# Reading two PSUM banks with one instruction: a reduction and an exponential over a pair of banks

## The chip, the cores and the metric

One core of one Trainium2 chip runs the whole kernel. The time is that of one execution on the device, in microseconds (us); the kernel before was run three times for it, and once more under the hardware profiler.

## What is computed

Two transformer blocks over 16 batches of 256 tokens, 128 channels each. Every block normalizes its input, runs an attention and a mixture of 8 experts (top 2) on it, and adds attention times silu(experts) to the input. Layer 0 has a causal attention with two softmaxes per head whose difference is taken; layer 1 has a window of 128 keys. Cut to the part around the change:

```python
# layer 0: 16 heads of size 8, causal, two score sets
att1 = softmax(where(causal, q1 @ k1.T * scale, -inf))
att2 = softmax(where(causal, q2 @ k2.T * scale, -inf))
y = (att1 - lam * att2) @ v            # then a norm over each head, then @ c_w
# layer 1: 16 heads of size 8, keys t-127 .. t
attn = softmax(q @ window(k).T / sqrt(8))
ctx = attn @ window(v)
```

## The kernel before

The kernel runs its stages one after another: layer norm, router, experts, attention, twice. The change lies in `build_attention` alone, which is built for each layer.

**Scores twice.** The attention computes the scores of a batch twice. The first pass is row by row (queries on the partitions): VectorE takes the maximum of each row of a head (`search`, L1277), and the negated maximum, the shift, is turned and written by DMA as two more rows into the stacked queries in SBUF (`fill_shift`, L935). The second pass, for the following batch's turn, is transposed (keys on the partitions) and has the shift already in the sum, so that ScalarE only has to take exp (`exp`, L1182) into `probs`, from which TensorE weighs the values (`weigh`, L1062).

**Units and banks.** A batch has UNITS units: 12 in layer 0 (A = 2 score sets), 6 in layer 1. In unit n of a step TensorE fills two banks `s_bank[0..1]` with scores for the maximum of a batch further on (AHEAD is 4 units plus a batch in layer 0, 3 plus a batch in layer 1), and two banks `t_bank[0..1]` with transposed scores of this batch, the matmuls of the two kinds alternating (`both_scores`, L1042, called for i = 0 and i = 1). A PSUM bank has 512 fp32 columns on each of 128 partitions. Matmuls L986 add the masks, L987 the products. There are 16, 20 or 24 of them in a unit that has both kinds.

**Who waits for whom.** `s_full` and `t_full` are counted up once per bank, as are `s_free` and `t_free`: before TensorE fills bank i of unit n it waits until VectorE and ScalarE have read bank i of unit n - 1, not the other one. The wait is

```python
lone_wait(pe, s_free, b * BANKS + (2 * m + i - 1))
lone_wait(pe, t_free, step * BANKS + (2 * n + i - 1))
```

**The order within a step.** All engines run the same written-out order, step by step and unit by unit, and every queue is in order. After the scores of unit n TensorE does in that unit: `weigh` (16 matmuls, L1077 and L1080) in units n = 0 and 1 (for the last group of the step before) and in n = 3, 4, 6, 7, 9, 10 of layer 0 and n = 3, 4 of layer 1; and the general work of the table ORDER. In layer 0: two turnings of weighed values at n = 2 (L1088), the projection of v at n = 4 (L975), of queries and keys at n = 5 and 6 (L968), the turned shift (L1103) and two more turnings at n = 8, and at n = 11 the turned rows (L1096, which waits for GpSimd) and the output projection (L1112). In layer 1: qk at n = 0 and 1, turnings at n = 2, the shift at n = 3, v and rows at n = 4, out at n = 5. ScalarE copies each of these results out of PSUM after the exponentials of the same unit. VectorE's order in a unit is: maxima, then `negate` (L1290), `twice_silu`, `split_shift` (L1306), `divide` (L1316) and the parts of `split` (L1265). In layer 0 `divide` is at n = 3 (second score set of the batch before) and n = 9, and the parts of `split` (L1269, L1272, L1275, 1024 columns wide) at n = 7, 8, 9.

**Two loops beside the units.** In layer 0 GpSimd normalizes the rows of the batch before (`head_norm`, L832: from L854 to L867), which begins after the `divide` of n = 3 and is awaited by L1096 at n = 11. In layer 1 the stacked queries and keys are written by 12 DMAs per batch from SyncE's queue (`fill_stack`, L924, issues on L933), after `fill_shift` in the same queue; ScalarE's copy of the next projection (`copy_qk`, L1162) waits for them and stands ahead of the exponentials of unit n = 1.

Of the kernel before, what the change touches and what calls it, by code (L numbers as in the profile page):

```python
# [6 lines left out]
ALU = mybir.AluOpType  # L7
ACT = mybir.ActivationFunctionType
AX = mybir.AxisListType
# [5 lines left out]
P = 128  # L15
# [11 lines left out]
SCALE = 1.0 / math.sqrt(HD)  # L27
# [13 lines left out]
SLOTS = HEADS // 2  # L41
# [615 lines left out]
def build_attention(nc, R, D, layer):  # L657
# [8 lines left out]
    A = 2 if layer == 0 else 1  # L666
# [6 lines left out]
    UNITS = 6 * A  # L673
    BANKS = 2 * UNITS
# [23 lines left out]
    def has(step, name):  # L698

        if not isinstance(step, int):  # L700
            return True
        if name.startswith("qk"):
            return 0 <= step + 3 <= LAST
        if name in ("v", "shift"):
            return 0 <= step + 1 <= LAST
        if name in ("rows", "out", "last", f"turn{A - 1}0", f"turn{A - 1}1"):
            return 0 <= step - 1 <= LAST
        return 0 <= step <= LAST
# [3 lines left out]
    def maxima_of(step, n):  # L712

        batch, m = (step + 1, n + AHEAD) if n + AHEAD < UNITS else (step + 2, n + AHEAD - UNITS)
        if isinstance(batch, int) and not 0 <= batch <= LAST:
            return None
        return batch, m
# [8 lines left out]
    with ExitStack() as ctx:  # L726
        sem = lambda name: ctx.enter_context(nc.semaphore(f"at{layer}_{name}"))

        def sb(name, shape, dt=F32):
            return ctx.enter_context(nc.sbuf_tensor(f"at{layer}_{name}", shape, dt))  # L730
# [5 lines left out]
        maxima = sb("maxima", [P, QB, A * HEADS])  # L736
# [3 lines left out]
        probs = sb("probs", [P, 2, 3, 1024])  # L740
# [29 lines left out]
        s_full, s_free = sem("s_full"), sem("s_free")  # L770
# [3 lines left out]
        t_full, t_free = sem("t_full"), sem("t_free")  # L774
# [22 lines left out]
        stack = R.stack  # L797
        G = [R.ps[:, i, :] for i in range(2)]
        s_bank, t_bank = ([R.ps[:, 2 * u + i, :] for i in range(2)] for u in (1, 2))
        Y = [R.ps[:, 6 + i, :].rearrange("p (f s) -> p f s", f=2) for i in range(2)]  # L800

        def bank_of(step, name):
# [7 lines left out]
        def lone_wait(eng, s, value):  # L810

            if not (isinstance(value, int) and value <= 0):
                eng.wait_ge(s, value)
                eng.sem_inc(passed, 1)
# [144 lines left out]
        def _(pe):  # L959
# [35 lines left out]
            def scores_for_max(j, batch_r, n, i):  # L995


                a, r = divmod(n, 6)
                q, k = (stack_of(batch_r, a, tensor) for tensor in range(2))
                late = int(r >= 2)  # L1000
                per, w = 4 // (late + 1), P * (late + 1)
                if j >= per + 2:
                    return None
                h0 = (r - 2 * late) * per
                if not late:
                    fine, mask = one_block(0), R.mask_diag_q[:]
                elif layer == 0:
                    fine, mask = one_block(P), R.mask_diag_q[:, 0:2, :]
                else:
                    fine, mask = two_blocks, R.mask_late_q[:]  # L1010
                ins = score_matmul(j, s_bank[i], i, per, SHIFT_ROW, fine, mask,
                                   lambda m: q[:, h0 + m, late * P:(late + 1) * P], lambda m: k[:, h0 + m, 0:w])
                if j == per + 1:
                    ins.then_inc(s_full, 1)
                return ins
# [26 lines left out]
            def both_scores(step, r, n, i):  # L1042

                ahead = maxima_of(step, n)
                now = has(step, "now")
                if ahead:
                    b, m = ahead
                    if m == 0 and i == 0:
                        pe.wait_ge(stacked, b * LOADS + LOADS)
                    lone_wait(pe, s_free, b * BANKS + (2 * m + i - 1))  # L1050
                if now:
                    if n == 0 and i == 0:

                        pe.wait_ge(shift_in, step * SHIFTS + SHIFTS)
                    lone_wait(pe, t_free, step * BANKS + (2 * n + i - 1))
                for j in range(6):
                    if ahead:
                        scores_for_max(j, r + 1 if n + AHEAD < UNITS else r + 2, m, i)
                    if now:
                        scores(j, r, n, i)  # L1060

            def weigh(b, p, g, part):  # L1062

                a, group = divmod(g, 2)
                if part == 0:
                    pe.wait_ge(t_free, b * BANKS + 6 * (g + 1))

                    lone_wait(pe, y_free, b * GROUPS + (g - 1))
                pr = probs[:, g % 2]
                for late in range(2):  # L1070
                    for j in range(STRIPS):
                        h = group * 8 + part * 4 + j
                        i, m = 1 - j // 2, j % 2
                        strip = Y[g % 2][j * VW:(j + 1) * VW, part, :]
                        if not late:
                            at = i * 512 + m * SEQ
                            nc.tensor.matmul(strip, v[p][:, 0, h, :], pr[:, part, at:at + SEQ], start=True, stop=False)  # L1077
                        else:
                            at = i * 512 + (part * 2 + m) * P
                            last = nc.tensor.matmul(strip[:, P:SEQ], v[p][:, 1, h, :], pr[:, 2, at:at + P], start=False, stop=True)  # L1080
                last.then_inc(weighed, 1)
# [69 lines left out]
        def _(act):  # L1151
# [30 lines left out]
            def exp(b, n):  # L1182
                if n % 3 == 0:

                    lone_wait(act, weighed, b * (2 * GROUPS) + 2 * (n // 3 - 1))
                for i in range(2):
                    act.wait_ge(t_full, b * BANKS + (2 * n + i + 1))
                    nc.scalar.activation(probs[:, (n // 3) % 2, n % 3, i * 512:(i + 1) * 512], t_bank[i], ACT.Exp, scale=SCALE).then_inc(t_free, 1)  # L1188

            def copy_weighed(b, g):  # L1190
                act.wait_ge(weighed, b * (2 * GROUPS) + 2 * (g + 1))

                nc.scalar.copy(weighed_t[:, g // 2, g % 2, :, :], Y[g % 2]).then_inc(y_free, 1)  # L1193

# [69 lines left out]
        def _(dve):  # L1264
# [12 lines left out]
            def search(b, n):  # L1277
                a, r = divmod(n, 6)
                late = int(r >= 2)
                heads = 4 // (late + 1)  # L1280
                if n == 0:
                    lone_wait(dve, shift_ready, b)
                for i in range(2):
                    h0 = i * SLOTS + (r - 2 * late) * heads
                    dve.wait_ge(s_full, b * BANKS + (2 * n + i + 1))
                    by_half = maxima[:, late, :].rearrange("p (h a) -> p h a", a=A)
                    nc.vector.tensor_reduce(by_half[:, h0:h0 + heads, a], s_bank[i].rearrange("p (m k) -> p m k", k=P * (late + 1)),  # L1287
                                            AX.X, ALU.max).then_inc(s_free, 1)

            def negate(b, p):  # L1290
                dve.wait_ge(s_free, b * BANKS + BANKS)
                if layer:

                    nc.vector.tensor_scalar(maxima[:, 0, :], maxima[:, 0, :], R.no_outside[:, 0:1], None, ALU.max).then_inc(max_ready, 1)
                    dve.wait_ge(max_ready, b + 1)
                if layer == 0:
                    nc.vector.tensor_scalar(shift[p][:], maxima[:], -1.0, None, ALU.mult).then_inc(shift_ready, 1)
                else:

                    nc.vector.tensor_scalar(high[:], maxima[:], -1.0, None, ALU.mult).then_inc(round_chain, 1)  # L1300
                    dve.wait_ge(round_chain, b * 2 + 1)
                    nc.vector.scalar_tensor_tensor(out=low[:], in0=maxima[:], scalar=-1.0, in1=high[:], op0=ALU.mult, op1=ALU.subtract).then_inc(round_chain, 1)
                    dve.wait_ge(round_chain, b * 2 + 2)
                    nc.vector.tensor_tensor(shift[p][:], high[:], low[:], ALU.add).then_inc(shift_ready, 1)
# [67 lines left out]
def build(nc, D):  # L1372
    D["list_in"] = nc.dram_tensor("list_in", (TILES * P, C), F32).ap()
    D["list_out"] = nc.dram_tensor("list_out", (TILES * P, C), F32).ap()
    with ExitStack() as ctx:
# [38 lines left out]
        for layer in range(2):  # L1414
            build_layernorm(nc, R, layer)
            build_router(nc, R, layer)
            build_experts(nc, R, D, layer)
            build_attention(nc, R, D, layer)
# [37 lines left out]
```

## Time and profile before

| | us |
|---|---|
| median of 3 runs | 1562.79 |
| lowest and highest | 1559.96, 1567.36 |
| the profiled execution | 1560.15 |
| its span (first to last instruction) | 1558.4 |

Busy shares of the span: TensorE 69%, VectorE 51%, ScalarE 49%, GpSimd 42%. The attention of layer 0 runs from about 327 us to 890 us with its tail, that of layer 1 from about 1194 us to the end; between and before them lie the experts. In the rows below, PE is TensorE matmuls, PEld its weight loads, DVE VectorE, ACT ScalarE, POOL GpSimd, SP SyncE.

### The profile page before, as it was taken

What the parts mean: (1) busy time and instruction counts of PE and PEld (TensorE: products, weight loads), DVE (VectorE), ACT (ScalarE), POOL (GpSimd) and SP (SyncE); (2) the same over time, 40 slices, a digit from 0 to 9 for tenths busy, and PEclk for the clock granted to TensorE, in tenths of its full rate; (3) what the DMA queues carried; (4) which work ended last, traced back from release to release, by engine and by line L of the source; (5) the groups of instructions that cost most, each with busy time, mean ns of one, the idle gap of its engine ahead of it and who ended that gap; (6) DMA issues with size and microseconds to landing.
All of it is one profiled execution on the core that took longest, in us unless ns stands there. A gap on an engine that the chain in (4) does not pass through costs nothing. (4 is left out here: it accounts for less than half of the span.)

```text
span 1558.4 us, 39725 instructions
## 1 busy us (share of the span) xinstructions
PE 1080.5 (69%) x12282; PEld 821.1 (53%) x12282; DVE 797.8 (51%) x1739; ACT 756.5 (49%) x1764; POOL 652.9 (42%) x868
## 2 busy tenths in 40 slices
PE   1400899858888788888888233009996678888886
PEld 1400899835655556555654122009996355555564
DVE  5411466447667666567562054115663555555561
ACT  2070456415667566676667022005553255555564
POOL 2277100010577677677767721760002013333344
PEclk9999999958899889898898555559998599999997
DMA  6061222132322232222400002312222222222220
GB/s 175 6 191 51 63 67 69 51 88 51 83 50 51 51 86 61 51 50 58 89 10 9 7 0 85 100 55 61 67 68 58 55 50 62 63 56 59 63 55 25
DMA packets 166094, 95.52 MB, mean 61 GB/s; under 512 B 18547, under 2 KB 159749, under 8 KB 165957
## 3 DMA queue, kind: packets, MB, share of 16 engines
q1 hardware_dynamic: 157764, 76.82, 19.0%
q0 software_dynamic: 8192, 16.79, 3.8%
q8 instruction: 96, 1.57, 0.4%
q14 instruction: 42, 0.34, 0.1%
HBM read 30.19 MB, written 24.64 MB: 35 GB/s over the span
## 5 line engine op out<-in xcount | busy, mean ns | idle before, releaser
L1287 DVE TENSOR_REDUCE at_maxima<-ps 128x2 f32<-128x512 f32 (+1 forms) x576 | 372.4, 685 | 224.2 <-PE ps L987 222.2
L1188 ACT ACTIVATE at_probs<-ps 128x512 f32<-128x512 f32 x576 | 322.4, 602 | 103.2 <-PE ps L987 98.3
L986 PE MATMUL ps<-tables 64*128 64x256 bf16 (+1 forms) x2304 | 232.6, 265 | 121.9 <-DVE at_maxima L1287 50.1
L615 ACT ACTIVATE ex_hid<-ps,ex_w 128x128 f32<-128x128 f32 x576 | 164.4, 368 | 251.0 <-PE ps L585 251.0
L987 PE MATMUL ps<-stack 64*128 64x128 bf16 (+3 forms) x3072 | 269.6, 262 | 0.0
L986 PEld LDWEIGHTS ps<-tables 64*128 64x128 bf16 x2304 | 96.1, 98 | 224.5 <-issue 189.8
L987 PEld LDWEIGHTS ps<-stack 64*128 64x128 bf16 (+1 forms) x3072 | 171.2, 102 | 9.1
L577 PE MATMUL ps<-ident,ex_rows 128*128 128x128 f32 x144 | 40.2, 279 | 195.2 <-DMA ex_rows<-list_in 195.1
L522 POOL DMA_INDIRECT list_in<-ex_rows,ex_slots x128 | 125.1, 977 | 100.9 <-DVE ex_slots L628 63.4
L646 DVE COPY ex_w<-ex_weights 128x1156 f32 x144 | 109.9, 763 | 106.4 <-issue 106.4
L585 PE MATMUL ps<-ex_rowsT,ex_w 128*128 128x128 f32 x1152 | 158.3, 282 | 0.1
L595 PE MATMUL ps<-ex_w,ex_hid 128*128 128x128 f32 x1152 | 153.6, 277 | 1.2 <-DVE ex_result L653 1.2
L877 POOL DMA_INDIRECT at_chosen_y<-list_out,at_slot x128 | 124.8, 975 | 55.6 <-issue 28.9
L585 PEld LDWEIGHTS ps<-ex_rowsT,ex_w 128*128 128x128 f32 x1152 | 143.1, 196 | 2.3 <-issue 0.7
L595 PEld LDWEIGHTS ps<-ex_w,ex_hid 128*128 128x128 f32 x1152 | 141.6, 194 | 1.5 <-issue 1.5
L1077 PE MATMUL ps<-at_probs,at_v 128*32 128x256 f32 x1536 | 130.9, 414 | 0.0
L577 PEld LDWEIGHTS ps<-ident,ex_rows 128*128 128x128 f32 x144 | 21.1, 146 | 197.0 <-issue 197.0
L898 POOL TENSOR_TENSOR at_s_rows<-at_s_rows,at_silu 128x256 f32<-128x256 f32 x32 | 23.5, 734 | 194.5 <-ACT at_s_rows L1229 194.1
L864 POOL TENSOR_TENSOR at_rstd<-at_stat,at_half 128x32 f32<-128x32 f32 x16 | 89.2, 5574 | 2.9 <-POOL at_stat L862 2.9
L1080 PE MATMUL ps<-at_probs,at_v 128*32 128x128 f32 x1536 | 80.7, 283 | 0.0
L626 DVE COPY ex_rows<-xn 128x128 f32 (+1 forms) x64 | 15.2, 237 | 123.8 <-DMA list_in<-ex_rows,ex_slots 123.2
L1269 DVE TENSOR_TENSOR at_whole<-at_whole,at_pieces 128x1024 f32<-128x1024 f32 (+1 forms) x32 | 31.1, 972 | 91.5 <-ACT at_pieces L1170 69.9
(166 smaller groups left out, 1555.6 us busy)
## 6 DMA issues: line engine op xcount, KB each, us to landing
stack<-at_pieces SPq DMA_DIRECT2D x192, 128.0 KB
stack<-at_pieces SPq DMA_DIRECT2D x192, 64.0 KB, 2.0
ex_rows<-list_in SPq DMA_DIRECT2D x144, 64.0 KB, 1.8
list_out<-ex_result SPq DMA_DIRECT2D x144, 64.0 KB, 1.5
list_in<-zero_tile SPq DMA_DIRECT2D x1, 4608.0 KB, 17.7
ex_weights<-in_L_w SPq DMA_DIRECT2D x4, 1024.0 KB, 7.4
ex_weights<-in_L_w SPq DMA_DIRECT2D x16, 256.0 KB, 7.1
x<-in_L_attn_x SPq DMA_DIRECT2D x4, 512.0 KB, 6.3
```

What stands on the lines that cost most here:

```text
L522: nc.gpsimd.indirect_dma_start(D["list_in"], bass.IndirectOffsetOnAxis(slots[q][k][:], 0), rows[q][:], None).then_inc(scattered[q], 16)
L585: last = nc.tensor.matmul(hid_ps[q % 2][:, hb * P:(hb + 1) * P], w[q][:, W1 + hb * P:W1 + (hb + 1) * P], rowsT[q % 2][:], start=True, stop ...
L595: last = nc.tensor.matmul(out_ps[q % 2][:, 0:C], hid[q % 2][:, hb, :], w[q][:, W2 + hb * C:W2 + (hb + 1) * C], start=(hb == 0), stop=(hb = ...
L615: last = nc.scalar.activation(hid[q % 2][:, hb, :], hid_ps[q % 2][:, hb * P:(hb + 1) * P], gelu, bias=w[q][:, B1 + hb:B1 + hb + 1])
L646: nc.vector.tensor_copy(w[q][:], weights[:, bass.ds(e, 1), :].rearrange("p o w -> p (o w)"))
L864: nc.gpsimd.tensor_tensor(rstd[:], stat[:], half[:], ALU.pow).then_inc(rstd_ready, 1)
L877: nc.gpsimd.indirect_dma_start(chosen_y[t][k][:], None, D["list_out"], bass.IndirectOffsetOnAxis(slot[:, i:i + 1], 0)).then_inc(gathered, 16)
L986: return nc.tensor.matmul(fine(bank, j), R.eye[tile, j, :], mask[tile], start=(j == 0), stop=True, skip_group_check=(j > 0))
L987: return nc.tensor.matmul(bank[:, j - 2, :], left(j - 2)[tile], right(j - 2)[tile], start=False, stop=True, skip_group_check=True)
L1077: nc.tensor.matmul(strip, v[p][:, 0, h, :], pr[:, part, at:at + SEQ], start=True, stop=False)
L1188: nc.scalar.activation(probs[:, (n // 3) % 2, n % 3, i * 512:(i + 1) * 512], t_bank[i], ACT.Exp, scale=SCALE).then_inc(t_free, 1)
L1287: nc.vector.tensor_reduce(by_half[:, h0:h0 + heads, a], s_bank[i].rearrange("p (m k) -> p m k", k=P * (late + 1)), AX.X, ALU.max).then_inc ...
```

## The change

One maximum over both s banks of a unit (an access pattern of 2 x heads x keys, 1024 columns) takes the place of two, and one exponential over both t banks (1024 columns) of two. `s_free` and `t_free` are counted once per unit, VectorE and ScalarE wait until both banks are full, and TensorE waits once, ahead of i = 0, until both banks of unit n - 1 have been read. `s_full` and `t_full` stay per bank.

```diff
+        s_pair, t_pair = R.ps[:, 2:4, :], R.ps[:, 4:6, :]
...
-                    lone_wait(pe, s_free, b * BANKS + (2 * m + i - 1))
+                    if i == 0:
+                        lone_wait(pe, s_free, b * UNITS + m)
...
-                    lone_wait(pe, t_free, step * BANKS + (2 * n + i - 1))
+                    if i == 0:
+                        lone_wait(pe, t_free, step * UNITS + n)
...
-                    pe.wait_ge(t_free, b * BANKS + 6 * (g + 1))
+                    pe.wait_ge(t_free, b * UNITS + 3 * (g + 1))
...
-                for i in range(2):
-                    act.wait_ge(t_full, b * BANKS + (2 * n + i + 1))
-                    nc.scalar.activation(probs[:, (n // 3) % 2, n % 3, i * 512:(i + 1) * 512], t_bank[i], ACT.Exp, scale=SCALE).then_inc(t_free, 1)
+                act.wait_ge(t_full, b * BANKS + 2 * (n + 1))
+                nc.scalar.activation(probs[:, (n // 3) % 2, n % 3, :].rearrange("p (i k) -> p i k", i=2), t_pair, ACT.Exp, scale=SCALE).then_inc(t_free, 1)
...
-                for i in range(2):
-                    h0 = i * SLOTS + (r - 2 * late) * heads
-                    dve.wait_ge(s_full, b * BANKS + (2 * n + i + 1))
-                    by_half = maxima[:, late, :].rearrange("p (h a) -> p h a", a=A)
-                    nc.vector.tensor_reduce(by_half[:, h0:h0 + heads, a], s_bank[i].rearrange("p (m k) -> p m k", k=P * (late + 1)),
-                                            AX.X, ALU.max).then_inc(s_free, 1)
+                h0 = (r - 2 * late) * heads
+                dve.wait_ge(s_full, b * BANKS + 2 * (n + 1))
+                by_half = maxima[:, late, :].rearrange("p (i h a) -> p i h a", i=2, a=A)
+                nc.vector.tensor_reduce(by_half[:, :, h0:h0 + heads, a], s_pair.rearrange("p i (m k) -> p i m k", k=P * (late + 1)),
+                                        AX.X, ALU.max).then_inc(s_free, 1)
...
-                dve.wait_ge(s_free, b * BANKS + BANKS)
+                dve.wait_ge(s_free, b * UNITS + UNITS)
```

## Rows read from the trace of the kernel before

**Rows 1.** Stretch, length, then busy us (x) of PE, PEld, DVE, ACT, POOL; clock; DMA.
```profile
419.99:805.75 385.76, 328.32 (x4721) 221.73 (x4721) 251.09 (x417) 256.19 (x512) 277.00 (x336) 0.88 0.25 58
1262.90:1496.70 233.80, 194.87 (x2400) 131.18 (x2400) 136.59 (x293) 134.82 (x326) 86.06 (x143) 0.94 0.23 59
547.50:551.40 3.90, 3.13 (x14) 2.53 (x16) 0.00 (x0) 0.58 (x1) 2.45 (x4) 0.50 0.85 213
```

**Rows 2.** TensorE's waits in twelve layer-0 steps: waiter, awaited: total us, times, longest.
```profile
PE ps L986 <- DVE at_maxima L1287: 18.5, 11, 2.1
PE ps L1096 <- POOL at_out_rows L867: 11.3, 12, 2.5
```

**Rows 3.** Timeline, TensorE, one layer-0 step: start us, us, instruction, count [idle before].
```profile
551.37 0.40 PE L986 MATMUL ps<-tables 64*128 64x128 bf16 x4
...
552.19 0.64 PE L987 MATMUL ps<-stack 64*128 64x256 bf16 x4
...
559.61 0.29 PE L986 MATMUL ps<-tables 64*128 64x128 bf16 x4
...
562.47 0.28 PE L986 MATMUL ps<-tables 64*128 64x128 bf16 x3
...
564.41 0.29 PE L986 MATMUL ps<-tables 64*128 64x128 bf16 x4
...
567.02 0.29 PE L986 MATMUL ps<-tables 64*128 64x128 bf16 x4
...
567.48 0.38 PE L987 MATMUL ps<-stack 62*128 62x256 bf16 x4
...
568.85 0.40 PE L986 MATMUL ps<-tables 64*128 64x256 bf16 x4 [0.20 <-ACT at_probs L1188]
...
571.82 0.39 PE L986 MATMUL ps<-tables 64*128 64x256 bf16 x4
...
572.38 0.39 PE L987 MATMUL ps<-stack 62*128 62x128 bf16 x6
...
576.99 0.28 PE L986 MATMUL ps<-tables 64*128 64x128 bf16 x3 [1.64 <-DVE at_maxima L1287]
...
579.36 0.66 PE L1096 MATMUL ps<-ident,at_out_rows 128*128 128x128 f32 x4 [1.15 <-POOL at_out_rows L867]
...
582.25 0.40 PE L986 MATMUL ps<-tables 64*128 64x128 bf16 x4
```

**Rows 4.** Timeline of the same step, VectorE's maxima of units 7 and 10.
```profile
567.56 1.29 DVE L1287 TENSOR_REDUCE at_maxima<-ps 128x2 f32<-128x512 f32 x2 [1.33 <-PE ps L987]
...
576.01 1.28 DVE L1287 TENSOR_REDUCE at_maxima<-ps 128x2 f32<-128x512 f32 x2
```

**Rows 5.** Groups by shape, 1024 columns: count | busy us, mean ns | idle before.
```profile
L174 DVE TENSOR_REDUCE ln_total<-ln_sq 128x8 f32<-128x1024 f32 x8 | 9.8, 1220 | 9.0 <-ACT ln_sq L194 9.0
...
L194 ACT ACTIVATE ln_sq<-xn 128x1024 f32<-128x1024 f32 x8 | 8.4, 1056 | 50.3 <-DVE xn L170 50.3
```

**Rows 6.** Timeline of the same step, GpSimd's first and last operation of the norm.
```profile
561.41 1.27 POOL L854 TENSOR_TENSOR at_y<-at_y 128x512 f32<-128x512 f32 x1 [3.00 <-DVE at_y L1336]
...
578.25 1.06 POOL L867 TENSOR_TENSOR at_out_rows<-at_y,at_rstd 128x512 f32<-128x512 f32 x1 [0.18 <-POOL at_rstd L864]
```

**Rows 7.** Timeline of layer 1, units 2 to 4 of a step.
```profile
1322.58 0.40 PE L986 MATMUL ps<-tables 64*128 64x256 bf16 x4 [1.94 <-ACT at_probs L1188]
...
1324.78 1.28 DVE L1287 TENSOR_REDUCE at_maxima<-ps 128x2 f32<-128x512 f32 x2
...
1325.76 0.40 PE L986 MATMUL ps<-tables 64*128 64x256 bf16 x4 [0.85 <-DVE at_maxima L1287]
...
1328.01 1.28 DVE L1287 TENSOR_REDUCE at_maxima<-ps 128x4 f32<-128x512 f32 x2
```

**Rows 8.** VectorE's maxima before layer 0's first full step (group, 330.7 to 347.8 us).
```profile
L1287 DVE TENSOR_REDUCE at_maxima<-ps 128x2 f32<-128x512 f32 (+1 forms) x18 | 11.6, 686 | 2.7 <-PE ps L987 2.7
```

**Rows 9.** Timeline of layer 1's last steps, one unit's maxima.
```profile
1516.22 1.29 DVE L1287 TENSOR_REDUCE at_maxima<-ps 128x2 f32<-128x512 f32 x2 [0.48 <-PE ps L987]
```

## Prediction

> **What bounds the kernel now.** I read the busy shares first, by stretch: in the steady steps of layer 0 TensorE is busy 328 of 386 us and VectorE 251, in layer 1 TensorE 195 of 234 [rows 1]. No engine is full, so the order of hand-offs decides. Next the waits: in twelve steps of layer 0 TensorE stands 18.5 us for maxima (11 times) and 11.3 us for GpSimd's normalized rows (12 times, 0.94 each) [rows 2]. Then one step in order of time. TensorE's own work paces most units: unit 4 takes 2.86 us (559.61 to 562.47), unit 6 2.61 (564.41 to 567.02). Unit 7, with little but scores and weighing in it, takes 1.83 us, and TensorE waits only 0.20 us after it [rows 3]. In that unit VectorE starts on the first bank at 567.56, while TensorE fills the second until 567.86 (567.48 + 0.38), and ends at 568.85, when TensorE has just begun unit 8 [rows 3, 4]. So the two banks of a pair overlap the engines: one is read while the other is filled or not yet needed. The whole step, 551.37 to 582.25, takes 30.88 us.
>
> Two loops run beside this. In layer 0 GpSimd works at the norm from 561.41 to 579.31 (578.25 + 1.06), 17.9 us, and TensorE waits 1.15 us for it in unit 11, after its scores ended at 578.21 [rows 3, 6]. In layer 1 TensorE stands 1.94 us ahead of unit 2 for an exponential [rows 7]; by the order of ScalarE's queue that exponential is behind a copy that waits for SyncE's twelve DMAs. Units 5, 0 and 1 of layer 1 therefore have some 2 us of cover.
>
> **What the change removes.** One reduction in two and one exponential in two. Two maxima back to back take 1.28 to 1.29 us [rows 4]. A 1024-column reduction, from SBUF, takes 1.22 [rows 5]. It is the nearest row in length and in kind, so I take 1.22 for the pair; the bounds are 1.22 and 1.29. An exponential pair should take about the 1.06 of the 1024-column square [rows 5], which is below 1.22 and starts at the same moment; I cost it at nothing where VectorE has nothing else to do, because the reduction hides it. The dropped waits of TensorE I cost at nothing too: they free a stall of up to 0.3 us between the banks, counted below for unit 11.
>
> The Trainium skill, VectorE: DVE Perf Modes, section "The TRN2 errata", gives a PSUM read on VectorE a fixed 120 cycles besides one per element at 0.96 GHz, so one instruction in place of two would save 0.125 us. The rows say 0.07, since the second of two reductions overlaps the first one's end. By the page's figure the sum below would be some 5 to 10 us smaller; I keep the row.
>
> **What it adds.** TensorE may not touch either s bank of unit n + 1 until the single reduction has ended, and that reduction may not begin until both banks of unit n are full. The unit's period gets a floor: scores of both banks, the reduction, and the way back to TensorE. The terms:
> - Scores of both banks without a stall: 0.84 us with 16 matmuls (567.02 to 567.86), 0.95 with 20 (571.82 to 572.77) [rows 3]; 1.06 with 24 by the same step, an estimate. In unit 0 the matmuls run at the lower clock and take 1.46 (551.37 to 552.83) [rows 3].
> - The reduction: 1.22.
> - The way back: a maximum starts at 1324.78, one bank takes 0.686 [rows 8], TensorE starts at 1325.76 [rows 7]: 0.29, say 0.3.
>
> The floors are 2.36 us (16), 2.47 (20), 2.58 (24) and 2.98 (unit 0). What is queued behind TensorE's wait is the scores, and behind them the weighing and the general work, which cannot move ahead. Unit by unit in layer 0, with the step shown [rows 3]:
> - Units 0 to 3: 8.24 us now (551.37 to 559.61), 2.98 + 2.36 + 2.58 + 2.47 = 10.39 after: +2.15.
> - Units 4 and 6: own work of 2.86 and 2.61 exceeds the floor: 0.
> - Unit 5: 1.94 now (562.47 to 564.41), 2.47 after: +0.53. Unit 7: 1.83 to 2.36: +0.53.
> - Unit 8: 2.97 now (568.85 to 571.82). Its second turning waits for ScalarE's shift copies, which are queued behind an exponential that now starts at about 1.1 us in place of 0.7. Bounds 0 and 0.4; I take +0.2.
> - Units 9 and 10: 5.17 now (571.82 to 576.99). VectorE's two maxima of unit 9 would run from about 572.5 to 573.8, and unit 10's start at 576.01 without idle [rows 4], so 2.25 us of its other work lie between. After: unit 9 takes 2.47; its reduction ends 2.17 into it; unit 10's starts 2.25 later, 1.95 into unit 10, and that unit takes 1.95 + 1.22 + 0.3 = 3.47. Sum 5.94: +0.77.
> - Unit 11: its scores take 1.22 now (576.99 to 578.21), 0.95 without the wait between banks: -0.27.
>
> That is +3.9 us. From it goes the cover: TensorE arrives later at the rows that it now awaits 0.94 us on average [rows 2]. Does GpSimd stay ahead? Its norm starts after unit 3's maxima, and those end 2.17 into the unit in place of some 1.95. From there to the end of unit 11's scores TensorE would need 0.3 + 2.86 + 2.47 + 2.61 + 2.36 + 3.17 + 5.94 + 0.95, about 20.7 us, GpSimd its 17.9 and VectorE's division of some 1.5 ahead of it, 19.4. So GpSimd is ready first and the cover is used up: **+3.0 us a step**, 13 steps between full ones: +39.
>
> The rest, by the same floor: before the first full step VectorE's maxima alone set the pace, nine pairs in 14.3 us of busy and idle time, 1.6 a pair [rows 8]. There the floor is about 1.1 (two banks at the lower clock, an estimate) + 1.22 + 0.3 = 2.6, +1.0 for 9 or 10 units: +9. The end of layer 0, exponentials without maxima: +3. Layer 1: its start, six units: +3. Its middle, 12 steps: TensorE starts unit 3 about 0.55 us later, but VectorE is busy until unit 3's maxima anyway (1324.78 to 1326.06, again from 1328.01 without idle [rows 7]), so the shift and SyncE's DMAs hardly move, and the 1.94 us at unit 2 takes up the rest: +2, bounds 0 and 6. Its last steps, where no loop waits: a unit's maxima come every 1.77 us (1.29 + 0.48) [rows 9] and would come every 1.05 + 1.22 + 0.3 = 2.6 (scores of 1.05 at layer 1's width, by bounds 0.95 and 1.1), some seven units: +6.
>
> **The sum.** 39 + 9 + 3 + 3 + 2 + 6 = +62 us against the profiled execution's 1560.15: 1622. The median of the runs lies 2.6 above that execution, so 1625.
>
> **The rivals.**
> - *Milder.* GpSimd's norm goes on setting layer 0's step, or TensorE's clock recovers in units 11 and 0 because it no longer stands ahead of the rows. Then a step gains only the start of the norm's delay, about +1.9, or loses the 1.2 us that the lower clock costs there: 13 x 1.8 + 12 = +35, 1598. For it: stalls at 0.50 clock are seen just there [rows 1]. Against it: the count above puts GpSimd 1.3 us ahead.
> - *The clock falls.* Every unit now has an idle of 0.5 to 0.9 us. If that keeps TensorE at 1.2 GHz, scores take 1.46 in place of 0.84 and eight floors of a step grow by 0.62: 13 x 5 + some 20 in layer 1, about 1710. Against it: around the idle 0.85 and 1.94 us in layer 1 the matmul groups keep their 0.40 us [rows 7], and that stretch runs at 0.94 [rows 1]; at the lower clock such groups last longer (0.64 against 0.38 [rows 3]). The Trainium skill, TensorE: Matmul & The Clock Gate, section "A second HAM failure mode: psum-queue depth-cycling", tells of a kernel whose short idle times between groups made the clock swing. By that rule this case would come true; the rows of layer 1 do not show it.
> - *Not slower.* TensorE's other work covers the reduction in every unit, and the shorter reading tells: 0.07 us on 288 pairs is at most -20 us, 1543, and with part of it covered, no change. It decides where the work after the scores reaches 1.5 us. Units 4 and 6 reach it; units 1, 2, 3, 5, 7 and 9 don't, with periods under 2.1 [rows 3].
>
> **How the numbers follow.** The floor with its covers 0.70; milder 0.13; the clock 0.08; not slower 0.09, of which within 0.5% (about what this kernel's runs can tell) 0.05 and faster 0.04. The range takes in the first two: below, cover in full and clock recovery with the start smaller, 1590; above, the reduction at 1.29 (+6), the way back or the queues of units 8 to 10 worse by 0.5 us each (+20), and the lower clock in a few more units (+20), 1670.
>
> **What would show it.** Right: TensorE's waits for maxima rise from 18.5 us in twelve steps to 60 or more; a plain unit's period is 2.3 to 2.5; one reduction lasts 1.22; the wait for rows in unit 11 is gone; layer 1's middle steps keep about 20 us. Wrong: unit 7 stays under 2 us (the floor is not there); L1096 still waits 1 us or more (GpSimd sets the pace); the granted clock in layer 0 falls below 0.8 from 0.88; or layer 1's steps grow by over a us, which would mean that SyncE's DMAs start later.

## The result and the profile after

| | before | after |
|---|---|---|
| median | 1562.41 us (4 runs, 1559.96 to 1567.36) | 1635.03 us (4 runs, 1633.72 to 1638.12) |
| ratio, 95% interval | | 1.0475 [1.0452, 1.0498] |
| span of the profiled execution | 1558.4 | 1632.5 |

The change makes the kernel 4.75% slower, +72.6 us. The forecast was 1625, with 1590 to 1670 around it.

The page of the changed kernel, its part with the costliest groups (line, engine, operation, count | busy us, mean ns | idle before):

```profile
L1288 DVE TENSOR_REDUCE at_maxima<-ps 128x4 f32<-128x1024 f32 (+1 forms) x288 | 352.2, 1223 | 324.9 <-PE ps L988 323.8
L1190 ACT ACTIVATE at_probs<-ps 128x1024 f32<-128x1024 f32 x288 | 295.1, 1025 | 252.7 <-PE ps L988 251.7
L987 PE MATMUL ps<-tables 64*128 64x256 bf16 (+1 forms) x2304 | 223.5, 263 | 228.7 <-DVE at_maxima L1288 144.0
```

The fused instructions do what they should: a reduction of 1024 columns takes 1.223 us and an exponential 1.025. But VectorE, whose busy time fell, is idle 324.9 us ahead of its reductions, and TensorE stands 144.0 us for them. They now wait for each other in turn.

Lines L986, L987, L1287 and L1188 of before are L987, L988, L1288 and L1190 here; L1088, L1096 and L1112 (the turnings and the output projection) are L1091, L1099 and L1115. Stretches of the changed kernel: the way to unit 11 of step 1 in layer 0, twelve steps of layer 0, its end, and eleven steps of layer 1 (columns as in [rows 1]):

```profile
327.44:435.41 107.97, 68.04 (x870) 43.97 (x871) 63.84 (x65) 43.07 (x66) 15.53 (x16) 0.75 0.19 46
435.41:865.73 430.32, 314.16 (x4721) 218.03 (x4722) 242.35 (x273) 238.76 (x368) 276.18 (x336) 0.92 0.24 54
865.73:919.72 53.99, 38.96 (x622) 25.69 (x623) 17.55 (x24) 34.26 (x51) 38.75 (x54) 1.00 0.05 12
...
1339.50:1565.12 225.62, 181.46 (x2289) 126.16 (x2290) 126.29 (x209) 126.31 (x243) 87.00 (x143) 0.95 0.24 60
```

The first two and the last of these stretches in the kernel before, cut at the same instructions (TensorE's first matmul of unit 11 in layer 0, of unit 5 in layer 1); the end of layer 0 took 56.66 us there:

```profile
327.47:413.85 86.38, 71.36 (x871) 45.39 (x871) 65.73 (x103) 45.49 (x89) 13.29 (x14) 0.79 0.24 58
413.85:798.61 384.76, 329.21 (x4721) 222.50 (x4722) 251.19 (x418) 255.65 (x512) 275.86 (x337) 0.87 0.26 60
...
1273.57:1496.73 223.16, 185.20 (x2289) 124.10 (x2289) 129.11 (x275) 127.82 (x309) 86.06 (x143) 0.95 0.24 61
```

The start of layer 0 costs 21.6 us, its twelve steps 45.6 (3.8 a step), its end gives back 2.7. Layer 1's eleven middle steps cost 2.5, its start and its end 3.9 and 5.5. That makes 76.3 us; the stretches between the layers and at the very end give back the remaining 2.2 of the spans' 74.1. The granted clock in the twelve steps did not fall, it rose from 0.87 to 0.92. With the same matmuls TensorE is busy 15.1 us less there (329.21 and 314.16) and idle 60.6 us more: part of what the new waits cost comes back through the clock.

One step's units 7, 10 and 11 in the changed kernel, TensorE:

```profile
527.40 0.29 PE L987 MATMUL ps<-tables 64*128 64x128 bf16 x4
...
529.80 0.40 PE L987 MATMUL ps<-tables 64*128 64x256 bf16 x4 [0.77 <-ACT at_probs L1190]
...
535.71 0.29 PE L987 MATMUL ps<-tables 64*128 64x128 bf16 x4 [0.81 <-DVE at_maxima L1288]
...
539.18 0.29 PE L987 MATMUL ps<-tables 64*128 64x128 bf16 x3 [1.84 <-DVE at_maxima L1288]
...
540.06 0.66 PE L1099 MATMUL ps<-ident,at_out_rows 128*128 128x128 f32 x4
```

and VectorE in the same units, then GpSimd:

```profile
528.27 1.22 DVE L1288 TENSOR_REDUCE at_maxima<-ps 128x4 f32<-128x1024 f32 x1 [1.39 <-PE ps L988]
...
536.53 1.22 DVE L1277 TENSOR_TENSOR at_pieces<-at_whole,at_pieces 128x1024 bf16<-128x1024 f32 x1
537.66 1.22 DVE L1288 TENSOR_REDUCE at_maxima<-ps 128x4 f32<-128x1024 f32 x1
```

```profile
537.20 1.46 POOL L868 TENSOR_TENSOR at_out_rows<-at_y,at_rstd 128x512 f32<-128x512 f32 x1 [0.18 <-POOL at_rstd L865]
```

Unit 7 now takes 2.40 us (1.83 before [rows 3]). Its reduction starts at 528.27, 0.87 into the unit, not at 0.54 [rows 4]; it ends at 529.49 and TensorE goes on at 529.80. The row names ScalarE's exponential, which ended at 529.51, a reminder that a wait for two is put down to one. In unit 11 TensorE no longer waits for the rows: GpSimd's last operation ended at 538.66, 1.4 us before TensorE came for them (1.15 us after it had come, before [rows 3, 6]).

TensorE's waits in the twelve steps (waiter, awaited: total us, times, longest), after and then before:

```profile
PE ps L987 <- DVE at_maxima L1288: 71.7, 81, 2.0
PE ps L1115 <- ACT at_yT L1204: 12.6, 12, 1.1
PE ps L1091 <- ACT at_shift_p L1219: 10.9, 11, 1.0
PE ps L987 <- ACT at_probs L1190: 9.4, 12, 0.9
```

```profile
PE ps L986 <- DVE at_maxima L1287: 20.0, 12, 2.1
PE ps L1096 <- POOL at_out_rows L867: 9.4, 12, 1.2
PE ps L1112 <- ACT at_yT L1202: 9.2, 12, 0.8
PE ps L1088 <- ACT at_shift_p L1217: 6.0, 11, 0.5
```

Waits for maxima rise from 20.0 us in 12 waits to 71.7 in 81; the 9.4 us for the rows are gone; two waits for ScalarE's copies grow.

### The profile page after: what moved, and what is told of

Its sections match the earlier page's. It is cut to its first block and busy times, and to the rows that moved or that the text cites. A ratio compares the mean times of both kernels' runs of the same rounds, so it can differ in the third digit from the quotient of the medians.

```text
span 1632.5 us, 37908 instructions
## 1 busy us (share of the span) xinstructions
PE 1051.3 (64%) x12282; PEld 813.3 (50%) x12282; DVE 782.2 (48%) x1451; ACT 731.3 (45%) x1476; POOL 653.3 (40%) x868
## 5 line engine op out<-in xcount | busy, mean ns | idle before, releaser
L1288 DVE TENSOR_REDUCE at_maxima<-ps 128x4 f32<-128x1024 f32 (+1 forms) x288 | 352.2, 1223 | 324.9 <-PE ps L988 323.8
L1190 ACT ACTIVATE at_probs<-ps 128x1024 f32<-128x1024 f32 x288 | 295.1, 1025 | 252.7 <-PE ps L988 251.7
L987 PE MATMUL ps<-tables 64*128 64x256 bf16 (+1 forms) x2304 | 223.5, 263 | 228.7 <-DVE at_maxima L1288 144.0
L987 PEld LDWEIGHTS ps<-tables 64*128 64x128 bf16 x2304 | 107.9, 98 | 316.3 <-issue 289.5
L988 PE MATMUL ps<-stack 62*128 62x256 bf16 (+3 forms) x3072 | 254.1, 260 | 3.6 <-issue 3.6
L988 PEld LDWEIGHTS ps<-stack 62*128 62x128 bf16 (+1 forms) x3072 | 166.9, 101 | 11.0 <-issue 4.2
L855 POOL TENSOR_TENSOR at_y<-at_y 128x512 f32<-128x512 f32 x16 | 20.4, 1275 | 176.2 <-DVE at_y L1337 175.9
```

Source lines behind the costliest of these rows:

```text
L987: return nc.tensor.matmul(fine(bank, j), R.eye[tile, j, :], mask[tile], start=(j == 0), stop=True, skip_group_check=(j > 0))
L988: return nc.tensor.matmul(bank[:, j - 2, :], left(j - 2)[tile], right(j - 2)[tile], start=False, stop=True, skip_group_check=True)
L1190: nc.scalar.activation(probs[:, (n // 3) % 2, n % 3, :].rearrange("p (i k) -> p i k", i=2), t_pair, ACT.Exp, scale=SCALE).then_inc(t_free, 1)
L1288: nc.vector.tensor_reduce(by_half[:, :, h0:h0 + heads, a], s_pair.rearrange("p i (m k) -> p i m k", k=P * (late + 1)), AX.X, ALU.max).then ...
```

## The experiments

The theory under test: a pair of banks lets TensorE fill one while VectorE reads the other, and reading both with one instruction ends that. Each unit gets a floor of scores, reduction and way back. Rivals: the wide instructions cost in themselves; each fused instruction costs its share; TensorE's clock; GpSimd's norm still sets the step. In the table below all ratios are to the kernel before on the same chip.

| | edit | us | ratio, 95% interval |
|---|---|---|---|
| 1 | maxima fused only | 1628.91 | 1.0415 [1.0381, 1.0449] |
| 2 | exponentials fused only | 1586.64 | 1.0140 [1.0096, 1.0184] |
| 3 | the change's waits, two instructions | 1646.20 | 1.0522 [1.0487, 1.0557] |
| 4 | only TensorE's wait is once | 1588.51 | 1.0156 [1.0123, 1.0189] |
| 5 | change, split part 3 later | 1606.50 | 1.0296 [1.0263, 1.0328] |
| 6 | before, split part 3 later | 1558.90 | 0.9994 [0.9976, 1.0012] |
| 7 | fused in covered units | 1561.82 | 1.0021 [1.0002, 1.0039] |
| 8 | fused in the others | 1644.81 | 1.0546 [1.0515, 1.0578] |
| 9 | change, TensorE waits per bank | 1656.83 | 1.0614 [1.0589, 1.0639] |
| 10 | the changed kernel again | 1636.29 | 1.0492 [1.0477, 1.0506] |

The kernel before had a median of 1563.83 beside 1 to 4, 1559.99 beside 5 to 8 and 1559.28 beside 9 and 10; 1 to 4 ran on one chip, 5 to 10 on another.

**1. Maxima fused only.**

```diff
-                    lone_wait(pe, s_free, b * BANKS + (2 * m + i - 1))
+                    if i == 0:
+                        lone_wait(pe, s_free, b * BANKS + 2 * m)
...
+                nc.vector.tensor_reduce(by_half[:, :, h0:h0 + heads, a], s_pair.rearrange("p i (m k) -> p i m k", k=P * (late + 1)),
+                                        AX.X, ALU.max).then_inc(s_free, 2)
```

> Only the maxima are read as a pair (TensorE waits once per unit on s, per bank on t; exponentials per bank). Theory, the lost overlap of two banks: the floor of a unit is scores 0.84 + reduction 1.22 + way back 0.3, and the exponential pair was hidden inside it, so nearly the whole cost is here: 65 to 75 us above the kernel before (it was +73 with both), ratio 1.042 to 1.048. Rival, each fused instruction costs its own share: about half, +36 us.

Measured: 1.0415, +65 us. As the theory had it: some nine tenths of the cost come with the maxima alone.

**2. Exponentials fused only.**

```diff
-                    lone_wait(pe, t_free, step * BANKS + (2 * n + i - 1))
+                    if i == 0:
+                        lone_wait(pe, t_free, step * BANKS + 2 * n)
...
+                nc.scalar.activation(probs[:, (n // 3) % 2, n % 3, :].rearrange("p (i k) -> p i k", i=2), t_pair, ACT.Exp, scale=SCALE).then_inc(t_free, 2)
```

> Only the exponentials are read as a pair. Theory: a floor of 0.84 + 0.05 + 1.02 + 0.14 = 2.05 us for a unit of 16 matmuls against some 1.6 to 1.8 before, partly covered by GpSimd's norm: about 1.0 us a step of layer 0, and some 3 us in each layer's last steps: +15 to +30 us. With the first kernel the two must add to more than the change's +73, since the floors hide each other. Rival, additive shares: +36 us here and +36 there.

Measured: 1.0140, +23 us. Equal shares for the two instructions are out. The two add to 88, not 73, as the theory wants, in which ScalarE's shorter floor hides behind VectorE's; the waits of the changed kernel agree (in layer 0's twelve steps TensorE's scores wait 81 times for maxima and 12 times for exponentials). But the sum alone does not prove it: kernels 1 and 2 each keep one of TensorE's two waits per bank, which the change drops, and kernel 9 will show that such waits have a cost of their own.

**3. The change's waits, two instructions each.** Both readers wait for both banks, TensorE waits once (its part of the edit is that of kernel 4, below).

```diff
...
-                    act.wait_ge(t_full, b * BANKS + (2 * n + i + 1))
+                    act.wait_ge(t_full, b * BANKS + 2 * (n + 1))
...
-                    dve.wait_ge(s_full, b * BANKS + (2 * n + i + 1))
+                    dve.wait_ge(s_full, b * BANKS + 2 * (n + 1))
```

> Two reductions and two exponentials per unit as before, but VectorE and ScalarE start only when both banks are full and TensorE waits once for both: the waits of the change without its wide instructions. Theory: the cost is the waits, and two reductions take 1.29 where one takes 1.22, so this is slower than the changed kernel by 0.07 us for each unit at the floor: +5 to +15 us over it, ratio 1.050 to 1.057. Rival, the wide access pattern across two banks costs in itself: near the kernel before.

Measured: 1.0522, +82 us. The cost is there without any wide instruction. So the wide access pattern is not what costs. Against two instructions under the same waits it looks worth 5 to 7 us (1.0475 and, in kernel 10, 1.0492), but the intervals overlap, so that gain is not shown. VectorE's pairs in this kernel:

```profile
530.10 1.29 DVE L1289 TENSOR_REDUCE at_maxima<-ps 128x2 f32<-128x512 f32 x2 [1.17 <-PE ps L987]
```

1.29 us where one instruction takes 1.22.

**4. Only TensorE's wait is once per unit.** The readers start on each bank as it fills.

```diff
-                    lone_wait(pe, s_free, b * BANKS + (2 * m + i - 1))
+                    if i == 0:
+                        lone_wait(pe, s_free, b * BANKS + 2 * m)
...
-                    lone_wait(pe, t_free, step * BANKS + (2 * n + i - 1))
+                    if i == 0:
+                        lone_wait(pe, t_free, step * BANKS + 2 * n)
```

> Instructions per bank, each starting when its own bank is full as before; only TensorE's wait is once per unit, for both banks. Theory: the first reduction starts 0.54 us into a unit of 16 matmuls and not 0.88, so the floor is 0.54 + 1.29 + 0.3 = 2.13 us and not 2.36: between a third and half of the cost, +20 to +35 us. Rival, TensorE's single wait is the whole of it and the start of the readers does not matter: +65 or more.

Measured: 1.0156, +25 us. A unit of 20 matmuls in it:

```profile
517.18 0.39 PE L986 MATMUL ps<-tables 64*128 64x256 bf16 x4
...
519.42 0.29 PE L986 MATMUL ps<-tables 64*128 64x128 bf16 x4 [0.50 <-DVE at_maxima L1289]
```

```profile
517.83 1.29 DVE L1289 TENSOR_REDUCE at_maxima<-ps 128x4 f32<-128x512 f32 x2 [0.31 <-PE ps L987]
```

The first bank is read from 0.65 us on (517.83), both are free at 519.12, TensorE starts at 519.42: 2.24 us, where the changed kernel has 2.5 to 2.6 for such a unit. Added in this order, the cost splits: about a third is TensorE's waiting for both banks to be free, two thirds (kernel 3 less kernel 4, 57 us) are the readers' waiting for both to be full. The other order, readers alone, was not run.

**5 and 6. One 1024-column subtraction of VectorE moved from unit 9 to unit 10 of layer 0**, in the changed kernel and in the kernel before.

```diff
-        SPLIT = {7: (0,), 8: (1,), 9: (2,)}
+        SPLIT = {7: (0,), 8: (1,), 10: (2,)}
```

> The changed kernel with one 1024-column subtraction of VectorE (the third part of split, layer 0) moved from unit 9 to unit 10, behind unit 10's maxima. Theory: in the changed kernel TensorE's own path through the units sets layer 0's step, and GpSimd's rows are ready 1.4 us before TensorE comes for them, so what is taken off unit 10 (3.46 to about 2.4 us) is gained whole: -1.0 us for each of 13 steps, -10 to -14 us. Rival, GpSimd's norm or the DMAs still set the step: 0 to -3 us.

> The same move in the kernel before. Theory: there TensorE already waits 0.94 us in unit 11 for GpSimd, so the 1.2 us taken off unit 10 turns into a longer wait for the rows: 0 to -4 us. Rival, TensorE's path sets the step here too: -12 us or more.

Measured: the changed kernel drops to 1.0296, 28 us less than in its own comparison (1.0475) and 30 less than kernel 10; the kernel before stays, 0.9994 with 1 inside the interval. TensorE's waits for the rows in the twelve steps of kernel 6, and units 10 and 11 in kernel 5:

```profile
PE ps L1096 <- POOL at_out_rows L867: 26.6, 12, 2.3
```

```profile
529.48 0.29 PE L987 MATMUL ps<-tables 64*128 64x128 bf16 x4 [0.81 <-DVE at_maxima L1288]
...
531.88 0.28 PE L987 MATMUL ps<-tables 64*128 64x128 bf16 x3 [0.77 <-DVE at_maxima L1288]
```

In the kernel before, what TensorE saves ahead of unit 11 it stands longer for GpSimd (26.6 us for 9.4): GpSimd's norm sets that step. In the changed kernel the same move is gained, so there TensorE's path sets it and the cover was used up. It is gained twice over, and the expectation (10 to 14 us) had only the first half. Unit 10 took 2.40 us in place of 3.46. And the twelve steps fell from 430.32 to 407.74, 1.9 a step, while their granted clock went from 0.92 to 0.96:

```profile
432.00:839.74 407.74, 299.83 (x4720) 207.87 (x4721) 246.72 (x274) 238.62 (x368) 275.68 (x336) 0.96 0.25 57
```

TensorE's busy time separates the two. Of the 22.6 us, 8.3 are idle time and 14.3 are shorter matmuls (299.83 for 314.16, the same instructions). TensorE's idle ahead of unit 11 went from 1.84 to 0.77 us, and the output projection that follows is where the difference is largest, in the changed kernel and then in kernel 5, the same step:

```profile
541.86 2.04 PE L1115 MATMUL ps<-wo,at_yT 128*128 128x128 f32 x8 [1.15 <-ACT at_yT L1204]
```

```profile
534.56 1.13 PE L1115 MATMUL ps<-wo,at_yT 128*128 128x128 f32 x8 [1.14 <-ACT at_yT L1204]
```

Over the twelve steps these matmuls take 411 ns each in the changed kernel and 319 in kernel 5. So the second half is TensorE running at its higher level (2.4 GHz) for more of each step; that the shorter idle ahead of unit 11 is what brings this about is the likely reading, and no run isolates it.

**7 and 8. Fused by unit.** Kernel 7 fuses where TensorE's own work is longer than the reduction, kernel 8 everywhere else.

```diff
+    FUSED = {4, 6} if layer == 0 else {4, 5}
...
+                if (n - AHEAD) % UNITS in FUSED:
...
+                if n in FUSED:
```

In kernel 8 the first line is

```diff
+    FUSED = set(range(UNITS)) - ({4, 6} if layer == 0 else {4, 5})
```

> The pair is read by one instruction only in the units whose other TensorE work is longer than the reduction (4 and 6 of layer 0, 4 and 5 of layer 1), per bank elsewhere. Theory: no floor is reached, so nothing is lost, and the shorter reading is worth 0.07 us at most in a few units: within 0.5% of the kernel before, 0 to -4 us. Rival, every pair costs: 24% of the change, about +15 us.

> The complement: pairs in all units but 4 and 6 of layer 0 and 4 and 5 of layer 1. Theory: the whole cost sits here, +68 to +76 us over the kernel before, as with the change. Rival, every pair costs alike: +55 to +60 us.

Measured: kernel 7 at 1.0021, 2 us above, where every pair costing alike would give 15; kernel 8 at 1.0546, +85 us. The cost lies in the units where the floor is reached; that every pair costs alike is out. Two misses. Kernel 7 was expected at 0 to -4 us and shows no gain from the shorter reading: where it is covered it is worth nothing either. And kernel 8 was expected at +68 to +76; with fewer fused units than the change it is slower than it by 8 to 11 us. It differs from the change in TensorE's waits, which stand ahead of each bank in all units, and this led to the next kernel.

**9. The change with TensorE's waits left per bank**, and 10, the changed kernel beside it. Both counts go up by two at once, so in i = 1 the wait is already met.

```diff
-                    if i == 0:
-                        lone_wait(pe, s_free, b * UNITS + m)
+                    lone_wait(pe, s_free, b * BANKS + (2 * m + i - 1))
...
-                    if i == 0:
-                        lone_wait(pe, t_free, step * UNITS + n)
+                    lone_wait(pe, t_free, step * BANKS + (2 * n + i - 1))
```

> The changed kernel, but TensorE keeps its waits ahead of each bank (both counts go up by two with one instruction, so the second pair of waits is met before it is reached). Kernel 8 showed units of 16 matmuls whose readers start 0.94 us into them and not 0.88. Theory: a wait that is already met costs TensorE about 0.06 us between the banks, on the path in some nine units a step: +7 to +12 us over the changed kernel, ratio about 1.053. Rival, met waits are free: the changed kernel's time within 3 us.

> The changed kernel itself on the same chip, to compare kernel 9 with: ratio 1.0475 as before, 1.045 to 1.050.

Measured: 1.0614 against 1.0492, 20.5 us more, beyond the expected 7 to 12. Met waits are not free here. A unit of 16 matmuls that begins at 619.61 (kernel 9):

```profile
619.61 0.28 PE L987 MATMUL ps<-tables 64*128 64x128 bf16 x4
...
622.08 0.40 PE L987 MATMUL ps<-tables 64*128 64x256 bf16 x4 [0.84 <-DVE at_maxima L1286]
```

```profile
620.56 1.23 DVE L1286 TENSOR_REDUCE at_maxima<-ps 128x4 f32<-128x1024 f32 x1 [1.41 <-PE ps L988]
```

Its reduction starts 0.95 us into the unit, 0.87 in the changed kernel, and the unit takes 2.47 us and not 2.40. Seven hundredths in nine units of 13 steps are 8 us. The whole is more because the other units lose too: on average over eleven steps units 1 to 10 are each 0.08 to 0.24 us longer than in kernel 10. The twelve steps differ by 11.3 us (442.38 and 431.1); the other 9 lie outside them and were not taken apart. Each dropped wait goes with a count of its own, and which of the two costs was not tried.

## Why the prediction was right

**The floor.** It was the likeliest case, and it is what happened. Predicted 2.36 us for a plain unit, measured 2.40 (unit 7); the terms: scores 0.84 and 0.84, reduction 1.22 and 1.22, way back 0.3 and 0.31 (529.49 to 529.80). A hand-off of some hundredths from TensorE to VectorE, left out of the sum, is the 0.03 left. Unit 10 was put at 3.47 and took 3.47 (535.71 to 539.18). Kernels 3 and 4 show the two waits of which the floor is made, kernels 7 and 8 that it costs only where it is reached.

**The cover.** The sum let the 0.94 us of waiting for GpSimd be used up, with GpSimd ready 1.3 us early; it was 1.4. Kernels 5 and 6 show both sides of it: GpSimd sets the step before, TensorE's path after.

**A step of layer 0, +3.0, measured +3.8.** The terms, unit by unit, can be laid beside the traces: means over eleven full steps, each unit taken from its first matmul of scores to the next unit's (419.99 to 775.19 before, 439.16 to 837.61 after).

| units | before | after | change | forecast |
|---|---|---|---|---|
| 0 to 3 | 8.09 | 11.21 | +3.12 | +2.15 |
| 4 | 2.89 | 2.63 | -0.26 | 0 |
| 5 | 1.96 | 2.52 | +0.56 | +0.53 |
| 6 | 2.62 | 2.62 | 0 | 0 |
| 7 | 1.83 | 2.42 | +0.59 | +0.53 |
| 8 | 2.98 | 3.37 | +0.39 | +0.2 |
| 9 and 10 | 5.27 | 6.04 | +0.77 | +0.77 |
| 11 with its cover | 6.66 | 5.42 | -1.24 | -1.21 |
| step | 32.29 | 36.22 | +3.93 | +2.97 |

The mis-sized term is units 0 to 3, one us too low. Three things make it up. Their floors sum to 10.70 and not 10.39 in nine of the eleven steps (+0.31), the hand-off's hundredths and some matmuls at the lower clock. The step taken as the base was slower in these units than the mean, 8.24 for 8.09 (+0.15). And two of the eleven steps take 13.5 us in them (+0.51). These two are the steps in which the loop, whose body holds four steps, starts over. There TensorE stands for nothing that the profile shows ("issue"), in the middle of unit 0's scores too:

```profile
550.16 0.40 PE L988 MATMUL ps<-stack 62*128 62x256 bf16 x2 [1.81 <-issue]
```

Such idle times of TensorE sum to 8.4 us before and 13.2 after in the twelve steps; kernel 10, the same program, has 11.9, and what causes them stays open. Unit 4 gained 0.26 where I had nothing: its scores take 1.11 us before and 0.84 after, without the wait between the banks.

In unit 8 the term is ScalarE's queue, as forecast: an exponential that begins later stands ahead of the copies that TensorE waits for (6.0 and 10.9 us in 11 waits), and the unit grew by 0.39, near the upper bound of 0.4.

Unit 11 came out to some hundredths, and that is in part luck. Three things not in the sum cancel: the copy ahead of the output projection is later (9.2 and 12.6 us in 12 waits, +0.27 a step), the turning of the rows is faster (1.07 and 0.78 us, at more of the higher clock), and the scores gain 0.39 and not 0.27. The step read for the forecast was also not typical: its unit 11 took 5.26 us, the mean was 6.66.

**The start of layer 0, +9 and one step of 3, measured +21.6.** The maxima alone went from 1.6 to 2.2 us a pair (nine pairs in 11.0 + 8.4 us), as forecast in kind and less in size:

```profile
L1288 DVE TENSOR_REDUCE at_maxima<-ps 128x4 f32<-128x1024 f32 (+1 forms) x9 | 11.0, 1223 | 8.4 <-PE ps L988 8.4
```

That is +5.1, where I had 9. What I had too low is all that follows it. The next stretch (355.62 to 370.24 before, 361.09 to 381.20 after), at a granted clock of 0.53 and 0.50, costs 5.5 us; the units in it that have both kinds of scores take 3.0 to 3.5 us each. The rest, up to the first of the twelve steps (43.61 and 54.21 us), costs 10.6; it ran at a granted clock of 1.00 before and 0.94 after.

**The end of layer 0, +3, measured -2.7.** Wrong in sign, small in size. There the granted clock was 1.00 where it had been 0.85: before, TensorE stood 6.4 us in two waits for the rows, after it 0.5 us in one. That the clock follows from this wait fits the rows and was not tested.

**Layer 1, +11, measured +11.9** (start 3 and 3.9, middle 2 and 2.5, end 6 and 5.5). For the middle the size is right and the reason only in part. I had TensorE later in unit 3 and the wait ahead of unit 2 shrinking by as much. It did not shrink: TensorE stands 19.5 us in 9 waits for exponentials before and 19.9 in 10 after. There was hardly a delay to take up: before the change the units already took 2.6 to 4.3 us each on average, where the floor was put at about 2.6, and none grew by more than 0.22.

**The waits dropped from TensorE, costed at nothing.** Kernel 9 puts them at 20 us. The sum was not hurt by it, because the scores' lengths that it used, 0.84 and 0.95, held with one wait; but to say that the dropped waits are worth nothing was wrong, and a change without that part would have cost 6.1%, not 4.9% (kernels 9 and 10).

**The rivals.** *The clock falls*: it rose to 0.92 in layer 0's steps and was 0.95 in layer 1's before and after. Idle times of 0.5 to 0.8 us ahead of most units did not bring it down; the rule of the Trainium skill, TensorE: Matmul & The Clock Gate, section "A second HAM failure mode: psum-queue depth-cycling", did not decide this case. *Milder* had two halves. That GpSimd goes on setting the step is excluded by kernels 5 and 6. That the clock recovers once TensorE no longer stands ahead of the rows did happen in part: the 15.1 us less of busy time are 1.25 a step, in unit 11 above all, while unit 0's scores still took 1.46 us in most steps. The sum left this out, and longer idle times than it had, units 0 to 3 above all, made up for it. *Not slower*: VectorE's busy time did fall, from 372.4 to 352.2 us for the maxima, and kernel 7 shows what that is worth where the floor is not reached: no gain (1.0021, interval 1.0002 to 1.0039). (Unit 2, named there with a period under 2.1 us, takes 2.17 in the step read; its floor of 2.58 is still above that.)

## What to carry to other kernels

Two buffers read by one instruction are one buffer. Before two readings are merged, work out the floor that is left (fill all, read all, way back) for each place in the schedule, and compare it with what the filling engine has to do there besides; merge only where that work is longer, and expect no more than the saved overhead, 0.07 us a pair here, which did not show in the time. Look also at who stands behind the merged instruction in its queue (the copies behind a later exponential). And take the base of a sum from the mean of many steps: the one step read here was short by more than a us, and the steps in which the loop starts over were not in it.

## What the runs showed beyond that

A wait of TensorE that is already met, with the count that goes with it, costs: two of each per unit made the readers start 0.07 us later in the unit shown, and the kernel 1.2 points slower (1.0614 against 1.0492). And a shorter idle time can pay twice: 1.07 us taken off one stall of 1.84 us came with 1.9 us a step, of which 1.2 are shorter matmuls, with the granted clock up from 0.92 to 0.96. Moving that one subtraction is worth 28 us in the changed kernel and nothing in the kernel before; no kernel tried was faster than the one before.
